# Moving one output tile and the C22 sum at the end of the last pass, and one C12 sum in every pass

## The reference

```python
qkv = silu(xn @ qkv_w.T)                              # 32 heads x (q, k, v) x 128
# per head, over blocks of 32 tokens, with a state kv:
scores = einsum('bhnd,bhmd->bhnm', cq, ck) * diag_decay
intra = einsum('bhnm,bhmd->bhnd', scores, cv)
inter = einsum('bhnd,bhde->bhne', cq * q_decay, kv)
kv = kv * block_decay + einsum('bhnd,bhne->bhde', ck * k_decay, cv)
attn = intra + inter                                  # then all heads side by side
normed = norm_w * attn * rsqrt(mean(attn * attn, -1) + EPS)
attention = sigmoid(xn @ gate_w.T) * normed @ out_w.T
# experts: softmax router, the best 2 of 8, rank 16, added to a base product
experts = einsum('ner,eor->no', h * combine, B) * SCALING + xn @ W_base.T + b_base
out = x + attention + experts
```

## Time and profile before

| | |
|---|---|
| median of three runs | 1065.02 us (1064.21 to 1065.18) |
| the profiled execution | 1064.77 us, its span 1063.0 us |
| TensorE clock granted | 1.000 of 2.4 GHz over the span |
| TensorE busy | 1055.1 us, 99% of the span, 6290 matmuls |
| VectorE busy | 642.6 us, 60% |
| ScalarE busy | 678.6 us, 64% |
| GpSimd busy | 633.5 us, 60% |
| DMA | 77.10 MB, 73 GB/s in the mean |

### The profile page before, as it was taken

The page is one execution under the profiler, slowest core; times in us unless marked ns, Lnnn a source line. Parts: engine busy times, 40 slices in busy tenths (PEclk is TensorE's granted clock), DMA queues, the critical chain, the costliest instruction groups (busy, mean ns, idle before and its releaser), DMA issues. The chain is left out here.

```text
span 1063.0 us, 20381 instructions
## 1 busy us (share of the span) xinstructions
PE 1055.1 (99%) x6290; PEld 935.8 (88%) x6290; DVE 642.6 (60%) x1196; ACT 678.6 (64%) x1465; POOL 633.5 (60%) x626
## 2 busy tenths in 40 slices
PE   8999999999999999999999999999999999999998
PEld 7998889888898888988899888988889888998897
DVE  6866564656546565565745656465655647456567
ACT  9677565766657565675756666576666757567542
POOL 5557563684737647485554847367463764647645
PEclk9999999999999999999999999999999999999999
DMA  8223222131222222131221312212121322123232
GB/s 297 83 64 90 60 66 60 52 89 41 65 55 87 76 50 74 24 99 55 68 55 56 87 40 61 60 55 84 44 68 47 105 63 64 55 55 90 70 105 80
DMA packets 124579, 77.10 MB, mean 73 GB/s; under 512 B 82784, under 2 KB 104544, under 8 KB 124512
## 3 DMA queue, kind: packets, MB, share of 16 engines
q1 hardware_dynamic: 124224, 75.84, 25.4%
q10 hardware_dynamic: 288, 0.52, 0.1%
HBM read 63.23 MB, written 13.11 MB: 72 GB/s over the span
## 5 line engine op out<-in xcount | busy, mean ns | idle before, releaser
L475 POOL TENSOR_TENSOR w_lo<-combo,w_hi 128x768 fp32r<-128x768 f32 (+1 forms) x128 | 164.8, 1294 | 120.6 <-ACT w_hi L671 120.3
L475 POOL TENSOR_TENSOR w_lo<-raw,w_hi 128x256 fp32r<-128x256 f32 (+1 forms) x128 | 131.7, 1032 | 83.4 <-ACT w_hi L671 82.2
L526 POOL TENSOR_TENSOR sum_sq<-sum_sq,square 128x512 f32<-128x512 f32 x64 | 82.8, 1293 | 100.2 <-ACT square L849 100.2
L1500 DVE TENSOR_TENSOR acc<-acc,outp 128x512 f32<-128x512 f32 x116 | 79.3, 684 | 65.8 <-PE outp L1934 65.7
L1932 PE MATMUL bank_q<-c_hi,w_hi 128*128 128x512 f32 x276 | 108.5, 393 | 0.0
L1933 PE MATMUL bank_q<-c_lo,w_hi 128*128 128x512 f32 x276 | 107.9, 391 | 0.0
L1934 PE MATMUL bank_q<-c_hi,w_lo 128*128 128x512 f32 x276 | 107.8, 390 | 0.0
L1932 PE MATMUL outp<-wo_hi,g_hi 128*128 128x512 f32 x250 | 98.0, 392 | 1.2 <-DVE acc L1500 1.2
L1933 PE MATMUL outp<-wo_lo,g_hi 128*128 128x512 f32 x250 | 97.7, 391 | 0.0
L1934 PE MATMUL outp<-wo_hi,g_lo 128*128 128x512 f32 x250 | 97.4, 390 | 0.0
L671 ACT ACTIVATE w_hi<-combo 128x768 fp32r<-128x768 f32 (+1 forms) x128 | 81.0, 634 | 20.8 <-issue 10.8
(11 more groups left out here) (321 smaller groups left out, 3462.2 us busy)
## 6 DMA issues: line engine op xcount, KB each, us to landing
raw<-w_chunks SPq DMA_DIRECT2D x165, 256.0 KB, 3.4
keys_dram<-cross SPq DMA_DIRECT2D x192, 32.0 KB, 1.6
keys_t<-keys_dram SPq DMA_DIRECT2D x96, 64.0 KB, 2.4
near_dram<-near SPq DMA_DIRECT2D x2, 2048.0 KB, 10.2
table<-near_dram SPq DMA_DIRECT2D x32, 128.0 KB, 2.1
fade<-near_dram SPq DMA_DIRECT2D x32, 128.0 KB, 3.2
y<-x SPq DMA_DIRECT2D x8, 256.0 KB, 3.0
out<-acc SPq DMA_DIRECT2D x7, 256.0 KB, 2.1
```

Of the source, the lines that this page charges most:

```text
L475: pool.tensor_tensor(piece(w_lo[i % 2], j), piece_source(i, j), piece(w_hi[i % 2], j).bitcast(F32), ALU.subtract).then_inc(wlo[j], 1)
L526: pool.tensor_tensor(sum_sq[:, s % 2, :], sum_sq[:, s % 2, :], square[:], ALU.add).then_inc(summed, 1)
L1500: dve.tensor_tensor(tile, tile, outp, ALU.add).then_inc(acc_done, 1)
```

## The change

Two pieces move, and nothing else changes: every engine has as many instructions as before, and the lists of ScalarE, GpSimd and SyncE are the same.

In the last pass TensorE issues product 3 of unit G01 ahead of output tile 11 instead of behind it, and VectorE takes the C22 sum of G01 right behind the refinement of batch 0's root, then the accumulate of tile 10, and then `result(0)`.

In every pass VectorE takes the low part of step 5's state and the gated low part of step 4 ahead of the C12 sum of unit QK3, instead of behind it.

```diff
                     probs_lo(5)
-                    make_c12(QK3)
                     state_low(5)
                     gated_lo(4)
+                    make_c12(QK3)
                     lo(QK3, "x")
                     lo(QK3, "q")
                     add_out(6)
...
                     inverse_root(0, 0)
+                    make_c22(G01)
+                    add_out(10)
                     result(0)
-                    add_out(10)
                     mean_square(1, 1)
                     result(1)
                     result(2)
-                    make_c22(G01)
                     inverse_root(1, 1)
...
                     rms(1, 1)
-                    prod(G01, 5)
+                    prod(G01, 5, 3)
                     output(11)
-                    prod(G01, 3, 4, 2)
+                    prod(G01, 4, 2)
                     output(12, 13, 14, 15)
```

## The result

| | before | after |
|---|---|---|
| median of 16 runs each | 1064.71 us (1064.09 to 1065.73) | 1066.95 us (1066.33 to 1067.94) |
| ratio, 95% interval | | 1.0021 (1.0015 to 1.0028) |
| the profiled execution | 1064.77 us, span 1063.0 us | 1066.75 us, span 1065.0 us |

The change costs 2.24 us. I had forecast a loss of 0.95 and 1065.8 us; 1066.95 lies in the range (1063.8 to 1067.3), at the bound of what I had called no change.

A forecast was written before the change was run, and what follows sets the result against it. TensorE, busy 99% of the span, was taken as the bound. Eight passes of +0.19 (+1.5) and the end's −0.57 gave +0.95 us: 1065.8 us, range 1063.8 to 1067.3.

The forecast's parts named there:

- what I had called no change: Whole program: about 0.2% (2.1 us) either way; below 1062.9 us counts as faster, above 1067.15 as slower.
- Attention stall: Step 5's attention product, every pass: its wait for `gated_lo(4)` goes, start 0.26 becomes 0.12 behind the cross product, −0.21 us.
- one of my signs of being wrong: Wrong if transposes don't wait, the eight passes differ, or the last half tile follows TensorE as closely as before.
- Idle VectorE and the transposes: Every pass: VectorE idles 0.40 before `gated_lo(4)`; step 6's transposes then wait for `fade_cross(5)`, making a pass 0.19 us longer.
- The slow release of 0.26: Step 6's transposes start 0.26 instead of 0.05 behind `fade_cross(5)`, making a pass 0.42 us longer.
- my slower rival: Release at the transposes as slow as at the attention product: 3.4 us in eight passes, 1067.6 us; chance 0.13.
- a cover I priced at nothing: ScalarE 0.57 late behind the C12 sum; TensorE's dependent steps lie behind two products and an output tile, so no cost.
- The last pass: Step 5 to step 6 in the eighth pass: taken as the others, +0.19 us.
- up to 0.57 a pass where that cover fails: TensorE steps needing late ScalarE results: upper price if the two products and output tile ahead don't hide the lateness.
- The end: End of the last pass: C22 sum and product 3 earlier, last half tile starting at 1059.26 instead of 1059.83.
- Gain 0.57, between 0.3 (the output transfers stand closer together) and 1.0: End of the last pass: 0.57 us saved; lower bound 0.3 from output transfers, upper bound 1.0 from TensorE's own gain.

The follow-up runs named there:

- the kernel with the second part alone: Kernel before with only state low and gated low moved ahead of the C12 sum, in all eight passes: 1066.86 us, ratio 1.0018.
- the kernel with `fade_cross(5)` earlier: Changed kernel with VectorE's `fade_cross(5)` ahead of the accumulate of output tile 6: 1066.99 us, ratio 1.0021 against the kernel before.
- `g_hi` earlier: Changed kernel with ScalarE's `gated_hi(4)` one place earlier, ahead of the high part of QK3's bank x: 1064.23 us, ratio 0.9995 against the kernel before.
- the move of p's addition alone: Changed kernel with VectorE's base addition of bank p second, ahead of banks x and r: 1065.90 us, ratio 1.0013 against the kernel before.
- the kernel with the early root: Kernel before with the last-pass reordering, batch 1's mean square and refinement earlier, and bank p's addition second: 1063.69 us, ratio 0.9990.

## Why the prediction was right, and where it was short

**Attention stall: right.** 0.26 became 0.12 in the seven passes ahead of the last. The last isn't like the others, as I had taken it to be: it has 0.40 before and still 0.22 after (0.12 in the kernel with the second part alone). "If the eight passes differ from each other" was one of my signs of being wrong, and it came true for this pass.

**Idle VectorE and the transposes: right, and to size.** I had 0.40 idle (0.32 in the row), the transposes 0.05 behind `fade_cross(5)` (762.36 to 762.41), and 0.19 more for a pass. The time from one cross product to the other, averaged over the six passes of the loop, went from 10.39 to 10.60: +0.21. The slow release of 0.26, which my slower rival needed, isn't there: the time came out on that rival's side of the forecast, and by other mechanisms. The Trainium skill (Perfetto Trace Analysis, Identifying Dependency Chains) says that an instruction that waits for several engines may have instructions with the further conditions inserted ahead of it. The trace agrees. In the kernel before, TensorE's queue gets past an instruction that waits for `gated_lo(4)` at 759.70, 0.04 behind the end of `gated_lo(4)`. Then comes a second one with two more conditions, at 759.82, and then the weight load with the fourth, at 759.89; the product starts at 759.92. So 0.22 of the 0.26 lie behind the late condition. Where the late condition stands in the weight load itself, the start follows at once: 0.05 at the transposes, and 0.06 at the state product of the kernel with `fade_cross(5)` earlier (767.18 to 767.24). The page gives no price; in these rows it is the instructions that stand between the late condition and the product.

**The faded keys, a cover I priced at nothing.** I saw that ScalarE would be 0.57 late and said its readers lie behind two products and an output tile. That cover exists in the kernel after only because the transposes hold TensorE first. The kernel with `fade_cross(5)` earlier shows the state product of step 6 held by the faded keys, for the same total. So +0.19 for a pass was nearly the right number (+0.21), but "the transposes wait" was only the first of two waits, and taking it alone away gains nothing.

**The last pass: failed by 0.3.** The same stretch of step 5 to step 6 went from 11.55 (1010.82 to 1022.37) to 12.05 (1012.01 to 1024.06) there, 0.5 where I took 0.19. In the trace of the second part alone it is 11.85, so the loss lies between 0.3 and 0.5: this pass scatters as the others don't. One piece is in TensorE's rows of the kernel after, at product 2 of unit QK0:

```profile
1017.81 0.39 PE L1934 MATMUL outp<-wo_hi,g_lo 128*128 128x512 f32 x1
1018.27 0.36 PE L1932 MATMUL bank_p<-bt_hi,hw_hi 128*128 128x256 f32 x1
```

```profile
1016.88 1.30 POOL L475 TENSOR_TENSOR w_lo<-raw,w_hi 128x512 fp32r<-128x512 f32 x1 [6.03 <-ACT w_hi L671]
```

0.46 between starts instead of 0.23. GpSimd's low part ends at 1018.18, just ahead of the late product; it had waited for ScalarE's high part, which is late behind the C12 sum. In the kernels with the second part alone and with `g_hi` earlier the same product stops by the same amount, 0.10 behind the end of the same low part. This is the "up to 0.57 a pass where that cover fails", in the one pass where it failed, at a price of 0.24. It is read from traces; no run takes it apart, and the rest of the 0.3 to 0.5 has no row of its own.

**The end: the step that failed.** Up to the last result each number held: product 3 1.06 behind product 5 with 0.78 idle (1.07 and 0.8), GpSimd's additions 0.63 later against product 5 (0.67), no wait on VectorE in the last results, the last half tile 0.65 earlier (0.57). What failed is the last line, "Gain 0.57, between 0.3 (the output transfers stand closer together) and 1.0": I took the last result's start as the end of the program. The transfers behind it weren't in the sum; I had named them as the lower bound and stopped at a gain. They ate all of it and 0.3 more: 18.9 became 19.2. That it was they is shown by the move of p's addition alone, which touches no instruction of TensorE and brings the end from 19.2 to 18.4 (1.05 less by the medians). The power took 1.45 beside two results, as I had kept it, and 1.02 where none runs beside it; the trace agrees with the page that I had weighed there (the Trainium skill, SBUF — State Buffer, Who interferes with whom).

**The sum.** Seven passes of 0.21 are 1.5, the last pass 0.5, the end 0.3: 2.3, measured 2.24 by the medians (2.0 between the two profiled spans, of which the one after reaches its first cross product 0.15 earlier). My 8 × 0.19 − 0.57 was short by 0.9 at the end of the program, 0.3 in the last pass and 0.1 in the others. The forecast held because its range took in the bounds, with 0.35 to spare; its middle had the wrong sign for one of two parts. For the end of the program that is luck.

## What to carry to other kernels

An instruction that is moved forward must have its inputs ready at the new place: 0.3 of idle time in front of it goes on to everything behind it, and it is cured at the engine that makes the input, not at the products that wait. When a wait is taken away, look for the next one at the same distance; here the faded keys stood right behind the transposes and took the whole gain. And the program ends when the last output has landed, not when the last result is made: work out what the transfers do when the results come closer together.

## What the runs showed that I had not expected

- Five output tiles and two halves filled the queue: 387 to 414 GB/s at a DMA share of 1.04 to 1.07 in three stretches of a microsecond after, against 247 to 313 in the same place before. From the last result to the end of the span that made 3.6 us instead of 2.7.
- A result on VectorE that reads two SBUF tiles can cost far more beside GpSimd's additions. In the kernel with the early root three took 3.11: the first two, ahead of the additions or at their very start, took 0.75 each, and the third 1.78; and the four additions took 6.44 instead of the 5.51 of the earlier trace rows. The early root moved the additions on to the results, and it paid all the same.
- A pass is very steady. Between the cross products of steps 0 to 4 and 6 and those that follow them, the means over the loop agree within 0.02 us in the traces of both kernels and of the experiments; only the stretch from step 5 to step 6 moves with the edits (10.39 before, 10.60 after, 10.58 with the earlier `fade_cross`, 10.23 with the earlier `g_hi`), and the mean of the one around the turn of the loop scatters by 0.15 between profiles. The last pass doesn't keep to this. A loss of 0.2 in a pass can be read to a tenth of itself, if it is read there.
